# A written calendar for cross attention and mixture attention: every due time drawn anew

## The reference

```
x = x + softmax(mask((LN(x) Wq)(ctx Wk)^T / sqrt(32))) (ctx Wv) Wo
h = LN(x)
gates, experts = top2(relu(mean(h) gw1^T + gb1) gw2^T + gb2)
W_p = Wm_p + sum_k gate_k * U_p[e_k] S_p[e_k] V_p[e_k]      for p in q, k, v, o
x = x + softmax(q k^T) v W_o^T + b_o,   q, k, v = h W_q^T, h W_k^T, h W_v^T (+ biases)
```

## Time and profile before

| | |
|---|---|
| timed runs | 1421.71, 1428.75, 1436.47 us; median 1428.75 |
| the profiled execution | 1419.3 us, span of its instructions 1417.5 us |
| mean granted clock of TensorE | 0.986 |
| TensorE busy | 1381.6 us, 97% |
| VectorE, ScalarE, GpSimd busy | 952.0 (67%), 861.4 (61%), 679.8 us (48%) |
| TensorE in the chain that ended last | 87% |

### The profile page before, as it was taken

The page is one execution under the profiler, slowest core; times in us unless marked ns, Lnnn a source line. Parts: engine busy times, 40 slices in busy tenths (PEclk is TensorE's granted clock), DMA queues, the critical chain, the costliest instruction groups (busy, mean ns, idle before and its releaser), DMA issues.

```text
span 1417.5 us, 17150 instructions
## 1 busy us (share of the span) xinstructions
PE 1381.6 (97%) x5704; PEld 699.8 (49%) x5704; DVE 952.0 (67%) x1687; ACT 861.4 (61%) x1499; POOL 679.8 (48%) x411
## 2 busy tenths in 40 slices
PE   8998999999999999999999999999999999999987
PEld 5545444545455554554555544555445454444432
DVE  4463567766767677766777677767777577666572
ACT  2426475866478663865568663976548665565652
POOL 2012143555446462546455463555534455465675
PEclk9999999999999999999999999999999999999999
DMA  7533223432524224532334324332245323233210
GB/s 264 132 88 101 60 67 113 124 77 46 144 70 105 75 54 126 138 91 48 76 118 110 76 59 136 104 89 67 54 121 144 76 46 106 56 96 85 82 39 30
DMA packets 78768, 130.81 MB, mean 92 GB/s; under 512 B 26375, under 2 KB 32135, under 8 KB 75608
## 3 DMA queue, kind: packets, MB, share of 16 engines
q1 hardware_dynamic: 74007, 128.55, 33.8%
q10 hardware_dynamic: 4672, 1.17, 0.4%
HBM read 66.08 MB, written 12.21 MB: 55 GB/s over the span
## 4 chain that ended last, share of the span: by engine, by line
PE 87%; ACT 5%; issue 2%; DVE 2%; POOL 2%; DMA 1%; SPq 1%; ACTq 0%; POOLq 0%; DVEq 0%
PE pj L1211 44%; PE scT L1296 8%; PE acc L1325 8%; PE sc L1268 7%; PE sc L1257 3%; PE pj L1241 2%; PE pj L1334 2%; PE scT L1289 2%; PE pj L1313 2%; PE pj L1305 2%; PE pj L1205 2%; ACT xhat L804 1%; PE pj L1196 1%; PE pj L1184 1%; ACT qs L887 1%
## 5 line engine op out<-in xcount | busy, mean ns | idle before, releaser
L919 ACT ACTIVATE probs<-scT 128x512 f32<-128x512 f32 x512 | 289.0, 594 | 300.6 <-PE scT L1296 294.8
L1042 DVE TENSOR_REDUCE negmax<-sc 128x1 f32<-128x512 f32 x512 | 338.2, 684 | 141.5 <-PE sc L1268 140.6
L778 POOL TENSOR_TENSOR probs_sum<-probs_sum,probs 128x1024 f32<-128x1024 f32 x128 | 300.1, 2366 | 56.8 <-ACT probs L919 56.8
L1069 DVE RECIPROCAL inv_sum<-pj 128x128 f32<-128x128 f32 x256 | 225.0, 921 | 57.6 <-PE pj L1334 40.7
L1268 PE MATMUL sc<-ks,qs 96*128 96x512 f32 x512 | 260.5, 541 | 3.1 <-DVE negmax L1042 1.5
L1211 PE MATMUL pj<-XT,Wqk 128*128 128x512 f32 x512 | 257.4, 599 | 0.6 <-DVE Wqk L1134 0.6
L1296 PE MATMUL scT<-qs,ks 99*128 99x512 f32 x512 | 251.8, 519 | 4.0 <-ACT probs L919 2.7
L774 POOL TENSOR_TENSOR probs_sum<-probs 128x1024 f32<-128x1024 f32 x64 | 151.4, 2372 | 171.7 <-ACT probs L919 171.7
L784 POOL TENSOR_TENSOR uv_stack<-UVS_sb,uv_stack 96x1024 fp32r<-96x1024 f32 x32 | 75.7, 2365 | 178.3 <-ACT UVS_sb L826 178.3
L1296 PEld LDWEIGHTS scT<-qs,ks 99*128 99x128 f32 x512 | 95.1, 191 | 118.4 <-ACT probs L919 59.0
L1268 PEld LDWEIGHTS sc<-ks,qs 96*128 96x128 f32 x512 | 97.5, 192 | 94.9 <-issue 49.7
(11 more groups left out here) (103 smaller groups left out, 1704.9 us busy)
## 6 DMA issues: line engine op xcount, KB each, us to landing
Wqk<-in_WmT SPq DMA_DIRECT2D x16, 1024.0 KB, 6.9
Wvo<-in_WmT SPq DMA_DIRECT2D x16, 1024.0 KB, 6.5
UVS_sb<-in_UVS SPq DMA_DIRECT2D x64, 192.8 KB, 3.4
qs<-stage_lo SPq DMA_DIRECT2D x136, 64.0 KB, 2.0
qs<-qs SPq DMA_DIRECT2D x34, 256.0 KB, 3.1
X<-in_x SPq DMA_DIRECT2D x8, 1024.0 KB, 5.9
ks<-stage_lo SPq DMA_DIRECT2D x128, 64.0 KB, 2.0
ks<-ks SPq DMA_DIRECT2D x32, 256.0 KB, 3.0
```

The source lines that it names most:

```text
L778: nc.gpsimd.tensor_tensor(probs_sum[:, pair], probs_sum[:, pair], probs[:, kt % 2, pair], ALU.add)\
L919: nc.scalar.activation(probs[:, kt % 2, jj, :], scT[:, ST[step], :], ACT.Exp, scale=SCALE)\
L1042: nc.vector.tensor_reduce(negmax[:, 0, n:n + 1], sc[:, SC[step], :], AX.X, ALU.max, negate=True)\
L1069: nc.vector.reciprocal(inv_sum[:, INV[use], at], pj[:, PJ[left_in(full)], at])\
```

## The change

All due times in `CALENDAR` and `OWN` are others. The order was searched anew, with a price put on each change of TensorE between wide products and those of 32 columns. `PERIOD`, the handlers, the instructions and their number, the buffers and the rules for waits are the same. Below are the lines that the prediction speaks of, in groups of equal kind.

```diff
 CALENDAR = {
-    "normalize": (-1775, 138),
-    "xpose": (-1734, -1732, -1712, -1710, 141, 141, 163, 163),
-    "q1": (-1699, -1685, -1674, -1663, -1653, -1636, -1593, -1581, -984, -957, -928, -909, -826, -754, -746, -720),
+    "normalize": (-1950, 47),
+    "xpose": (-1925, -1923, -1886, -1882, 50, 52, 57, 61),
+    "q1": (-1734, -1734, -1733, -1723, -1708, -1694, -1694, -1626, -985, -981, -974, -919, -775, -756, -733, -728),
...
-    "gate_top": (235,),
+    "gate_top": (98,),
...
-    "qk_split": (552, 683, 1229, 1267, 1475, 1687, 2227, 2353),
-    "qk_rows": (919, 773, 1317, 1353, 1778, 1739, 2284, 2360),
+    "qk_split": (566, 724, 1197, 1248, 1417, 1605, 2100, 2141),
+    "qk_rows": (909, 779, 1293, 1300, 1782, 1761, 2111, 2160),
...
-    "shift": (1339, 1901, 2375, 2899),
+    "shift": (1329, 1935, 2188, 2888),
...
-    "pv": (1586, 1615, 1860, 2110, 2174, 2226, 2359, 2380, 2589, 2596, 2735, 2911, 3110, 3268, 3376, 3426),
+    "pv": (1578, 1578, 1932, 2058, 2078, 2100, 2144, 2197, 2581, 2581, 2775, 2879, 3073, 3224, 3399, 3399),
...
-    "den": (1871, 2376, 2959, 3434),
+    "den": (1932, 2332, 2946, 3399),
...
 OWN = {
-    "context_keys": {(0, 0): -11084, (1, 0): -10576, (2, 0): -9150, (3, 0): -8881, (0, 1): -8717, (1, 1): -8570,
-        (2, 1): -1258, (3, 1): -1209},
-    "split_keys": {(0,): -8404, (1,): -808},
+    "context_keys": {(0, 0): -12841, (1, 0): -12776, (2, 0): -10667, (3, 0): -10521, (0, 1): -10353, (1, 1): -10169,
+        (2, 1): -3059, (3, 1): -2549},
+    "split_keys": {(0,): -9966, (1,): -1983},
...
-    "wm_load": {(7, 3): 18708, (0, 0): -327, (0, 1): 223, (0, 2): 718, (7, 1): 14706, (7, 0): 14531, (7, 2): 14385},
+    "wm_load": {(7, 3): 19912, (0, 0): -1152, (0, 1): 32, (0, 2): 489, (7, 1): 14741, (7, 0): 14324, (7, 2): 14339},
...
```

More of the change, by code:

```diff
@@ L56 @@
[L56 to L64, removed]
@@ new lines @@
+    "q1_split": (-1708, -1488, -902, -682),
+    "q1_rows": (-1707, -1156, -899, -465),
+    "q1_stack": (-1639, -1071, -875, -357),
+    "pick": (115,),
+    "uv_load": (120, 359, 441, 2843),
+    "csc": (-1464, -1444, -1420, -1358, -1071, -1051, -1041, -1036, -713, -705, -688, -659, -279, -242, -200, -188),
+    "cross_shift": (-1344, -1023, -651, -167),
+    "cross_shift_move": (-1292, -987, -646, -143),
+    "csT": (-1189, -1187, -1186, -1179, -954, -941, -934, -920, -594, -548, -481, -477, -100, -92, -79, -64),
@@ new lines @@
+    "cpv": (-1122, -669, -458, -55),
+    "cacc": (-1120, -661, -439, -38),
+    "cden": (-993, -632, -457, -58),
+    "cinv": (-987, -983, -978, -919, -574, -518, -482, -478, -447, -446, -409, -349, -57, -38, -36, -32),
+    "wm_load": (92, 394, 603, 3177),
+    "cdivide": (-821, -475, -220, -37, -28, -9, 4),
+    "out1": (-66, -62, -34, -23, -33, -32, -25, -17, -17, -15, -8, -6, 0, 0, 4, 4),
+    "residual1": (-16, -16, 7, 13),
+    "residual_bias": (943,),
+    "token_sums": (59, 59, 61, 61),
@@ L104 @@
+    "accout": (2067, 2516, 3006, 3436),
+    "den": (1932, 2332, 2946, 3399),
+    "inv": (1933, 1939, 1947, 1951, 2332, 2342, 2347, 2428, 2951, 2978, 2986, 2992, 3420, 3428, 3436, 3439),
+    "divide": (2501, 2799, 3458, 3506, 3529, 3550, 3566),
+    "out2": (3453, 3484, 3522, 3571, 3652, 3702, 3740, 3815, 3870, 3890, 3917, 3917, 3937, 3968, 3983, 3990),
+    "residual2": (3587, 3923, 3961, 3999),
 }
 OWN = {
-    "context_keys": {(0, 0): -11084, (1, 0): -10576, (2, 0): -9150, (3, 0): -8881, (0, 1): -8717, (1, 1): -8570,
-        (2, 1): -1258, (3, 1): -1209},
@@ new lines @@
+    "csc": {(0, 0, 0): -2532, (0, 0, 1): -2509, (0, 0, 2): -2373, (0, 0, 3): -2340, (0, 1, 0): -1871,
[4 rows of a table added]
+    "cross_shift": {(0, 0): -2096, (0, 1): -1436, (0, 2): -812, (0, 3): -689, (7, 1): 13231, (7, 2): 13588,
+        (7, 3): 14077},
+    "cross_shift_move": {(0, 0): -2048, (0, 1): -1428, (0, 2): -772, (0, 3): -669, (7, 1): 13234, (7, 2): 13588,
+        (7, 3): 14131},
+    "csT": {(0, 0, 0): -1948, (0, 0, 1): -1919, (0, 0, 2): -1863, (0, 0, 3): -1851, (0, 1, 0): -925, (0, 1, 1): -925,
[4 rows of a table added]
+    "cpv": {(0, 0): -1122, (0, 1): -722, (0, 2): -415, (0, 3): -134, (7, 0): 13116, (7, 1): 13569, (7, 2): 13780,
+        (7, 3): 14182},
@@ L251 @@
[L251 to L254, removed]
+    "residual_bias": {(7,): 15112},
[7 rows of a table added]
+    "qk_split": {(7, 0, 0): 14778, (7, 0, 1): 14962, (7, 1, 0): 15404, (7, 1, 1): 15616, (7, 2, 0): 16835,
+        (7, 2, 1): 18150, (7, 3, 0): 20338, (7, 3, 1): 20750},
+    "qk_rows": {(7, 0, 0): 15004, (7, 0, 1): 15085, (7, 1, 0): 15573, (7, 1, 1): 15617, (7, 2, 0): 19053,
+        (7, 2, 1): 19448, (7, 3, 0): 20725, (7, 3, 1): 20854},
@@ new lines @@
+    "den": {(7, 0): 19496, (7, 1): 21112, (7, 2): 22271, (7, 3): 24832},
+    "inv": {(7, 0, 0): 19797, (7, 0, 1): 19901, (7, 0, 2): 19924, (7, 0, 3): 20162, (7, 1, 0): 21238,
+        (7, 1, 1): 21674, (7, 1, 2): 22089, (7, 1, 3): 22193, (7, 2, 0): 22511, (7, 2, 1): 23712, (7, 2, 2): 23806,
+        (7, 2, 3): 24376, (7, 3, 0): 25138, (7, 3, 1): 25393, (7, 3, 2): 25545, (7, 3, 3): 26189},
+    "divide": {(7, 0, 0): 21491, (7, 1, 0): 22387, (7, 2, 0): 24445, (7, 3, 0): 25294, (7, 3, 1): 25646,
+        (7, 3, 2): 29017, (7, 3, 3): 29299},
```

129 lines of the change are left out of this document (50 added, 79 removed), and 192 rows, old and new, of tables (CALENDAR, OWN).

## The result

The kernel after takes 1443.61 us (median of four runs, 1440.06 to 1447.29), the kernel before 1426.22 us in the four runs beside it (1421.71 to 1436.47). The ratio is 1.0115, 95% interval 1.0073 to 1.0156: slower by a little over 1%, 17 us, where 2 us less were forecast. The profiled execution takes 1445.2 us, its span is 1443.4 us, 25.9 us more than the span before; the mean granted clock is 0.975 (before 0.986).

The account below looks back on a forecast made before the run. The prediction took TensorE's own work to bound the middle, with waits worth removing in head and tail. Its terms, -3.2 + 6.5 - 4.1 - 1.1 = -1.9 us, took 1428.75 to 1426.9, say 1427 us; range 1415 to 1440.

Parts of the forecast that it names:

- Stays, -3.2: Whole kernel: ten fewer unbroken stays among TensorE's 32-column products (144 to 134), at 0.32 us each: -3.2 us.
- Middle transposes, +6.5: Middle batches: waits at third transpose, `shift` and `den` sum to 1.95 us for 0.88, +1.1 in six batches: +6.5 us.
- What comes next on TensorE has longer distances than 2 us to what it needs, so nothing is added behind it: Middle batches, behind the waits at transposes, `shift`, `den` and `q1`: later steps have enough slack, so 0 us more.
- The head, -4.1: Start of the kernel: four places where the order changes shorten TensorE's waits, together -4.1 us.
- (a): Head: `q1` of batch 0, about 1.1 us late for the `XT` copies, gets `context_keys` products ahead of it: -1.1 us.
- (b): Head: `qk` 0.0.0.0, 0.8 us late for the bank of `weff` (0,0,2), gets a whole product in between: -0.8 us.
- (d): Head: `cross_shift_move` (0,2) comes 2 us of TensorE work earlier before its `csT`: -1.0 us, ends -3 and +2.
- (c): Head: `split_keys` 1 moves out of the cross-attention scores; transposes of maxima lose their waits in part: -1.2 us.
- The tail, -1.1: End of the kernel: GpSimd's last adds precede `divide`, `den` (7,3) comes 1.26 us sooner, 0.2 given back: -1.1 us.
- (B): Rival, middle batches: they don't wait longer, so the 6.5 us are not paid: 1420.5 us, chance 0.20.
- (D): Rival, head and tail: the head gains its upper end, the tail loses a clock fall: 1419 to 1414 us, chance 0.10.
- (C): Rival, middle batches: the clock falls in every one after the three waits: 1437 to 1447 us, 1437 taken, chance 0.20.

Follow-up runs that it names:

- e2: The kernel after with the load of the next batch's keys (`context`) back at its old due time, -2070 for -1726: 1433.61 us, ratio 1.0045 to the kernel before.
- g3: The kernel before with only the keys' load (`context`) moved, from -2070 to -1645, behind both stacks of head group 3: 1467.16 us, ratio 1.0255.
- e3: The kernel after with the order of the kernel before up to the first transpose of batch 1: 1438.81 us, ratio 1.0112 to the kernel before.
- f2: The kernel before with only the keys' load moved, from -2070 to -1726, still ahead of both stacks of head group 3: 1427.85 us, ratio 1.0014.
- e4: The kernel after with batch 0's load of `Wvo` moved back behind the small UV loads: 1446.85 us, ratio 1.0162 to the kernel before.
- e1: The kernel after with the four row copies `qk_rows` (b,3,1) moved behind the fourth `XT` copy: 1463.23 us, ratio 1.0269 to the kernel before.
- h1: The kernel after with before's head order, keys' and `Wvo` loads moved back, row copies behind `XT` copies, and the gate's exponential sooner: 1445.61 us, ratio 1.0131.
- g2: The kernel after with before's head order, keys' and `Wvo` loads moved back, `hiddenB` as a copy, row copies behind the gate's scaling: 1471.84 us, ratio 1.0311.

## Why the prediction was wrong

*Stays, -3.2: not contradicted, and not shown by itself.* Ten stays fewer are a matter of counting; no run changed them alone. With the waits and the clock taken out, TensorE's own work comes to some 3 us less, an estimate from the distances between starts in the two traces.

*Middle transposes, +6.5: right in place and kind, a little large.* Of the three waits of 1.95 us a batch, that at the transposes (0.55) didn't appear, `shift` came some 0.2 us late (0.35), and `den` 1.4 us (1.05), of which 1.23 us are idle. 1.6 for 0.88 is +0.7 a batch, some +4.3 us in six.

*"What comes next on TensorE has longer distances than 2 us to what it needs, so nothing is added behind it": the step that failed, first part.* The distances were counted in TensorE's work, without SyncE's queue. `csc` (b,0,0) needs a stack that is issued behind a megabyte of weights; that megabyte now stands behind the keys, and the keys behind the stack of head group 3, which waits for the row copies. The move of `context` past `qk_stack` was not costed at all, a term of 10 us put at nothing without a reason. Its waits make 1.49 + 0.38 + 0.53 + 3.65 = 6.05 us of idle time. Against e2, whose order on TensorE is the same, the half clock behind the last costs 4.1 us more; e2's time is 10 us less by this load alone, and g3 puts 40 on.

*"VectorE and ScalarE ... a long piece of theirs in the wrong place": second part.* `gate_hidden` moved from ahead of GpSimd's additions to beside them. Its price in the trace before was 0.28 us, and the one entry of 1.33 us, in batch 7, went unasked. 0.64 us in five batches and 0.99 in one, 4.2 us. That it waits for the addition is shown by where it ends, in every profile; what it costs the kernel is read from the trace, since no experiment took it away.

*The head, -4.1: the step that failed, third part.* The waits went much as forecast: none is left ahead of the first `q1` (a), `qk` 0.0.0.0 (b) and `csT` (0,2,0) (d); those for the maxima (c), 0.87 and 0.32 us, became 0.67 and 0.67. The whole went the other way, by the clock, which the head's sum left out. Seven profiles with exactly before's order up to batch 1's transposes have these at 108.4 to 112.8 us, mean 111.1, and half clock in the cross attention for 3.4 to 13.7 us; five with after's order there, give or take the keys of batch 1, at 113.6 to 115.4, mean 114.6, with 23.9 us in each: +3.5 us. The timed runs of e3, which put the old order back, don't confirm it (ratio 1.0112 for 1.0115). Nor does the order decide by itself: f2 and g3 share one order up to that point, before's without the keys of batch 1, and f2's profile has the 23.9 us (114.1), g3's 6.8 us (112.0). Which of the moved steps makes the long half clock the rule, (c), (d) or the loads, stays open. One more stands among them that neither the section on the change nor the prediction names: the `warm` steps, products whose result nobody uses and which fill TensorE's waits in the head, alone kept their due times, while the steps around them came earlier. Before, the first stands ahead of the transpose of the maxima of group 1 (53.75 us); after, it stands behind it, at 63.70 us, when the clock had been down since 58.5. No run tests them. Further on `weff` (0,2,0), which the four places of the head left out, adds 2.6 us, and in two of the four profiles that keep this order of loads a half clock; e4's profile is without either, its times don't confirm it.

*The tail, -1.1: the mechanism came, the gain didn't.* The additions stand back to back and `den` (7,3) starts 1.0 us sooner counted from the last `shift`; but its own wait grew, and the clock fell behind it:

```profile
1427.02 1.78 PE L1334 MATMUL pj<-probs_sum,ones 128*32 128x512 f32 x8 [2.83 <-POOL probs_sum L778]
```

```profile
1427.24:1430.65 3.41, 3.41 (x11) 0.89 (x4) 1.74 (x3) 0.00 (x0) 1.32 (x2) 0.50 0.00 0
```

One wait of 1.76 us had become one of 2.83 us. From the last `shift` to the start of the last `out2` product it is 35.1 us before and 35.5 after.

*The sum as it came.* Head +7.0 (2.8 of it scatter), the stage with `weff` (0,2,0) +4.6, `csc` with its half clock +10.2, `den` less the old wait +4.3, `hiddenB` +4.2, stays some -3: 27 us, for 25.9 between the two profiles and -1.9 forecast.

*The rivals.* (B) is out, since the wait of `den` came, and so is (D), since the head lost. (C) had the right size, 1437 and above, by luck: the `den` wait left the clock at 1.00; it fell behind the one long wait for a DMA, 3.65 us. The prediction's own sign to look for, a clock under 1.00 from 300 to 1200 us, came true (0.99).

## What to carry to other kernels

When an order is changed, walk the DMA queue as its own engine: list what each small transfer that TensorE waits for has in front of it, before and after, and count a load as moved when it passes one of these, however little its due time changes. Look too at how far ahead of the small transfer the last large one is issued, since any change that brings the two together can make it late (after, e1, g3, h1). A wait that is removed brings the next step nearer to its data, so it pays only if that data has slack: e1, g2 and h1 each removed the wait they aimed at and ended 18 to 45 us slower than the version they started from. Where two engines share something, a duration holds only for what the other engine was doing beside it.

## What the runs showed of the hardware

The same 128x128 fp32 operation of VectorE took 0.28 us beside an idle GpSimd and 2.08 us behind a 128x1024 addition of GpSimd begun 0.37 us earlier, in two forms; wherever it began beside such an addition it ended 0.08 to 0.09 us behind it. A 256 KB copy inside SBUF, the second part of the query stack, landed 3.1 to 5.0 us after its issue where a load of one megabyte had been issued 3.7 to 5.4 us ahead of that stack, and after 4.3 to 9.8 us where this was 0.5 to 2.7 us. The start of the kernel, before batch 1, scatters by 4 us between executions of the same order (108.4 to 112.8 us in seven profiles). Idle waits of TensorE of 1.2 us in every middle batch left its clock at full; one of 3.65 us was followed by half clock for 10 us, one of 2.83 us in e2 by none.
